# Four stages on one core: another order of GpSimd's and VectorE's steps, the last samples' work as an order written out by hand, and the filter's spectrum in five steps

## The chip, the cores and the metric

The kernel runs on one core of a Trainium2 chip. Time is device microseconds of one execution, start to end; the number compared is the median of the runs.

## What is computed

Eight samples of 512 tokens by 128 channels pass through four stages, and each stage adds the layer norm of its result to its input:

```python
x = x + _layernorm(_L0_attn_ref(_layernorm(x), ...))   # six layers
x = x + _layernorm(_L0_ffn_ref(_layernorm(x), ...))    # spiking
x = x + _layernorm(_L1_attn_ref(_layernorm(x), ...))   # state space
x = x + _layernorm(_L1_ffn_ref(_layernorm(x), ...))    # gated
```

- Stage 1: six layers of linear attention with eight heads (softmax of the queries over a head's 16 channels, of the keys over the tokens) and a leaky-ReLU feed-forward of width 512.
- Stage 2: `h = relu(x Wfc)^2`, `y = h Wproj`, then the number of spikes of a leaky integrator in five steps, which is a count of how many of five levels `y` exceeds.
- Stage 3: `u = x Win + b`, a causal convolution of each channel with a kernel built from 64 states, done through a spectrum (transform, product, inverse), and `y Wout + b`.
- Stage 4: with the token before, `xk = mu_k x + (1 - mu_k) x_prev` and `xr` likewise; `out = sigmoid(xr Wr) * (relu(xk Wk)^2 Wv)`.

## The kernel before

Everything is in fp32 and stays in on-chip memory between load and store. `X` holds the eight samples and `XI` the running input of stage 1. Each of the five engines has its own program, written in order; semaphores join them. PSUM has eight banks, each with a fixed role: `pXT`, `pQ`, `pK`, `pX2`, `pH` (two), `pY`, `pW`.

Stage 1 is a pipeline over 48 items (six layers by eight samples). In step `n`, item `n` does its keys and queries, item `n-1` its attention, item `n-2` its second norm, item `n-3` its feed-forward. Product after product is placed on TensorE so that something else runs while a result goes over ScalarE or VectorE. In a step, GpSimd does: the join of the statistics (`join`), the power that gives the second norm's scale (`RSTD`, L790), the subtraction of the queries' maximum (`QB`, L877), the power for the first norm of the next item (`RSTD`, L797), and the queries' division (`QB`, L886). VectorE begins a step with the second scaling (`XR2`, L1315), then the scaled merge (`MM`, L1477), then the transpose of the queries' blocks (`QS`, L1481), then `XTL` (L1484). ScalarE scales the next item's input (`XR`, L956) once L797 has run, and TensorE transposes that at the start of the next step.

From step 44 on, the later stages of the samples come in. Sample `v` is at stage `k` of ten in step `44 + v + k`: `at(n, k, operation)` calls it. So one sample enters with each step and all five engines' orders repeat, up to step 60. The waits that guard the reuse of a bank come from `freed(name, count)` with a formula over the step.

Beside this, the convolution's kernel is built during stage 1: GpSimd and ScalarE make 16 chunks of powers, TensorE multiplies two slices of them in each of 32 steps (`kernel_slice`) into `pW`, ScalarE copies them out in steps 41 and 42, `CENTRE` is step 43, and VectorE combines them (`butterfly`) up to step 46. The filter's spectrum, 18 products of 128x128, is made in steps 48 and 49 into `pK` and `pQ`.

In stage 4, the previous token's part is folded into the weights: `WK1 = mu_k Wk`, `WK2 = (1 - mu_k) Wk`, and TensorE multiplies both with the sample `SH`, the second shifted by a token:

```python
mm(pY[:, :], WK1[:, :], SH[:, 1:1 + SEQ], True, False)
mm(pY[:, :], WK2[:, :], SH[:, 0:SEQ], False, True)
```

## Time and profile before

| | |
|---|---|
| time, three runs | 846.48, 844.92, 845.98 us; median 845.98 |
| profiled execution | 846.16 us, of which 844.3 from the first to the last instruction |
| mean granted TensorE clock | 0.981 |
| busy | TensorE 791.0 us (94%), VectorE 662.4 (78%), ScalarE 584.7 (69%), GpSimd 462.1 (55%) |

A matmul of fp32 is two rows in the profile (`x` counts them), so the 32 rows of `SH,WK` are 16 products. An `Lnnn` is a line of the kernel; helpers (`mm` is L317, `transposes` L327, `stats` L1194 and L1197, ScalarE's `copy` L908 and `normalise` L913) have one line for many uses, and the tile names tell them apart. Names lose their numbers: `XR2` reads `XR`, `WK1` reads `WK`; tiles that share the large buffer read `BIG`. Step 44 begins at 552.5 us, where GpSimd divides item 43's queries; step 48 begins at 626 us.

### The profile page before, as it was taken

How to read it: one execution, taken by the hardware profiler on the slowest of the kernel's cores; microseconds unless marked ns; L12 is line 12 of the kernel's file. 1: busy time of each engine (PE TensorE's matmuls, PEld its weight loads, DVE VectorE, ACT ScalarE, POOL GpSimd, SP SyncE). 2: the span in 40 equal slices, each digit the busy share in tenths (PEclk: the TensorE clock that was granted, in tenths of full speed). 3: DMA queues.
4: the chain of work that ended last, by engine and by line, in shares of the span. 5: the costliest groups of instructions: out<-in, count | busy, mean ns of one | idle time of the engine just before them, and what ended most of it. 6: DMA issues, size and time to landing. Idle time of an engine off the chain costs nothing.

```text
span 844.3 us, 16194 instructions
## 1 busy us (share of the span) xinstructions
PE 791.0 (94%) x5354; PEld 687.8 (81%) x5354; DVE 662.4 (78%) x1937; ACT 584.7 (69%) x1244; POOL 462.1 (55%) x740
## 2 busy tenths in 40 slices
PE   7689999999999999999999999989999999998864
PEld 3468888999899989999899998878888887877752
DVE  4668788888788788788878787897875799999951
ACT  3466777787787777777777777778777657756353
POOL 6888556565576536544554445543454355566543
PEclk9799999999999999999999999999999999999996
DMA  9200000100000000100001000000000000000001
GB/s 258 94 0 2 1 1 1 39 1 2 1 26 14 2 2 1 38 2 1 1 2 39 1 1 1 1 1 3 1 1 1 2 1 2 2 14 26 14 14 38
DMA packets 19729, 13.70 MB, mean 16 GB/s; under 512 B 2488, under 2 KB 18495, under 8 KB 19647
## 3 DMA queue, kind: packets, MB, share of 16 engines
q1 hardware_dynamic: 19646, 12.67, 5.2%
q8 instruction: 44, 0.72, 0.4%
q14 instruction: 39, 0.31, 0.1%
HBM read 10.57 MB, written 2.10 MB: 15 GB/s over the span
## 4 chain that ended last, share of the span: by engine, by line
PE 76%; POOL 9%; DVE 7%; issue 4%; ACT 3%; DMA 0%; POOLq 0%; ACTq 0%; DVEq 0%
PE PS L317 68%; PE PS L327 8%; POOL XI L767 2%; ACT BIG L913 1%; POOL QB L877 1%; POOL RSTD L790 1%; POOL RSTD L797 1%; POOL RX L758 1%; ACT XR L956 1%; DVE QSM L1537 1%; DVE STATS L1273 1%; DVE STX L1258 1%; POOL R L725 1%; DVE ST L1194 0%; DVE XR L1315 0%
## 5 line engine op out<-in xcount | busy, mean ns | idle before, releaser
L317 PEld LDWEIGHTS PS<-W,HL 128*128 128x128 f32 x1536 | 194.1, 191 | 13.3 <-issue 5.3
L317 PE MATMUL PS<-W,HL 128*128 128x128 f32 x1536 | 202.0, 275 | 0.0
L969 ACT ACTIVATE HL<-PS 128x512 f32<-128x512 f32 x192 | 109.3, 593 | 14.5 <-PE PS L317 10.6
L779 POOL TENSOR_TENSOR JOIN<-STATS 128x8 f32<-128x8 f32 (+1 forms) x48 | 12.2, 254 | 159.0 <-DVE STATS L1273 159.0
L317 PE MATMUL PS<-X2H,W1L 128*128 128x512 f32 x192 | 91.6, 477 | 2.6 <-issue 2.2
L1138 ACT ACTIVATE EK<-PS,NKM 128x512 f32<-128x512 f32 x48 | 33.0, 688 | 76.7 <-DVE NKM L1498 76.7
L886 POOL TENSOR_TENSOR QB<-QB,QRC 128x512 f32<-128x512 f32 x48 | 50.9, 1061 | 56.5 <-DVE QRC L1540 56.5
L956 ACT ACTIVATE XR<-XI,RSTD 128x128 f32<-128x128 f32 x192 | 61.5, 393 | 25.4 <-POOL RSTD L797 25.3
L317 PE MATMUL PS<-X2H,W1H 128*128 128x512 f32 x192 | 76.2, 397 | 0.0
L317 PE MATMUL PS<-X2L,W1H 128*128 128x512 f32 x192 | 76.0, 396 | 0.0
L1273 DVE BATCH_NORM_STATS2 STATS<-XI 128x6 f32<-128x128 f32 x352 | 75.5, 277 | 0.1
L327 PE MATMUL PS<-ID,XR 128*128 128x128 f32 x384 | 61.2, 283 | 9.4 <-ACT XR L956 9.4
L724 POOL TENSOR_SCALAR VE<-MV 128x4 f32<-128x4 f32 x56 | 13.5, 241 | 102.8 <-DVE MV L1197 101.4
L725 POOL TENSOR_TENSOR R<-VE,MHALF 128x4 f32<-128x4 f32 x56 | 59.8, 1069 | 4.7
L1509 DVE STREAM_TRANSPOSE QB<-QF 128x512 f32<-128x512 f32 x48 | 34.2, 712 | 34.5 <-ACT QF L908 34.5
L317 PE MATMUL PS<-MM,QS 128*128 128x128 f32 x384 | 54.7, 286 | 4.3 <-DVE MM L1477 2.8
L327 PEld LDWEIGHTS PS<-ID,XR 128*128 128x128 f32 x384 | 44.4, 144 | 15.1 <-ACT XR L956 12.4
L797 POOL TENSOR_TENSOR RSTD<-JOIN,MHALF 128x4 f32<-128x4 f32 x40 | 55.2, 1381 | 0.0
L1495 DVE TENSOR_TENSOR XI<-PS,XI 128x512 f32<-128x512 f32 x48 | 33.1, 690 | 27.6 <-PE PS L317 27.6
L317 PEld LDWEIGHTS PS<-MM,QS 128*128 128x128 f32 x384 | 47.6, 194 | 8.2 <-DVE MM L1477 4.5
L877 POOL TENSOR_TENSOR QB<-QB,QMX 128x512 f32<-128x512 f32 x48 | 51.7, 1078 | 4.5 <-DVE QMX L1513 4.5
L1320 DVE TENSOR_TENSOR X2L<-X2F,X2H 128x512 fp32r<-128x512 f32 x48 | 36.0, 749 | 23.2 <-ACT X2F L961 23.1
(215 smaller groups left out, 2167.2 us busy)
## 6 DMA issues: line engine op xcount, KB each, us to landing
W<-in_w SPq DMA_DIRECT2D x12, 256.0 KB
X<-in_x SPq DMA_DIRECT2D x8, 256.0 KB, 4.6
out<-X SPq DMA_DIRECT2D x8, 256.0 KB, 2.3
QKV<-in_qkv SPq DMA_DIRECT2D x6, 192.0 KB, 2.8
FWD<-in_fwd SPq DMA_DIRECT2D x1, 1024.0 KB, 5.5
INV<-in_inv SPq DMA_DIRECT2D x1, 1024.0 KB, 8.1
WO<-in_wo SPq DMA_DIRECT2D x6, 64.0 KB
FWDX<-in_fwdx SPq DMA_DIRECT2D x1, 256.0 KB, 6.5
```

Source lines behind the costliest of these rows:

```text
L317: return nc.tensor.matmul(o, l, r, start=start, stop=stop, skip_group_check=True)
L327: last = nc.tensor.transpose(o[:, j * P:(j + 1) * P], i[:, j * P:(j + 1) * P], ID[:, :])
L725: return pool.tensor_tensor(RS[k][:, :], VES[k][:, :], MHALF[:, 0:TILES], ALU.pow)
L797: power = pool.tensor_tensor(RSTD[:, 0:TILES], variance, MHALF[:, 0:TILES], ALU.pow)
L877: pool.tensor_tensor(heads(QB[:, :]), heads(QB[:, :]), QMX[:, :].unsqueeze(2).broadcast_to([P, 32, DH]), ALU.subtract).then_inc(s["q_sub"], 1)
L886: pool.tensor_tensor(heads(QB[:, :]), heads(QB[:, :]), QRC[:, :].unsqueeze(2).broadcast_to([P, 32, DH]), ALU.mult).then_inc(s["q_nrm"], 1)
L956: last = nc.scalar.activation(o[:, j * P:(j + 1) * P], tile(src, b, j), ACT.Copy, scale=r[:, first + j:first + j + 1])
L969: nc.scalar.activation(HL[f][:, :], pH[f % 2][:, :], ACT.Prelu, alpha=LEAK).then_inc(s["hl"], 1)
L1273: last = nc.vector.bn_stats(STATS[:, first + j, :], tile(src, b, j))
L1320: tt(X2L[:, :], X2F[:, :], X2H[:, :].bitcast(FP32), ALU.subtract).then_inc(s["x2l"], 1)
L1495: tt(xo, pQ[:, :], xo, ALU.add).then_inc(s["resid1"], 1)
L1509: nc.vector.transpose(QB[:, :], QF[:, :]).then_inc(s["q_blk"], 1)
```

## The change

- GpSimd, each step of stage 1: the first norm's power comes right behind the join, and the second norm's power behind the queries' subtraction.
- VectorE, each step: merge and `QS` come ahead of the second scaling.
- Three kernel slices a step instead of two, so the kernel is complete in step 30; `CENTRE` is step 33, and the spectrum is made in steps 37 to 41, two units a step, all into `pW`.
- From step 44 on, the loop over steps ends. Each engine has a written-out list of calls for what is left, with the counts that guard a bank beside the call. A sample no longer enters with each step: samples 1 and 2 come close together, as do 4 and 5, and the last items' feed-forwards are taken as fast as they come.
- Stage 4: the mixture with the previous token is made on the activations. ScalarE copies the transposed sample twice, scaled by `1 - mu` (`SHK`, `SHR`), and VectorE adds `mu x` from PSUM in two instructions (`blend`). TensorE then multiplies once, not twice: one product fewer of 512 columns and four fewer of 128 for each sample.
- The normed results go into `XI` in place of five separate tiles, so some waits on their reuse go. The output's weight and bias of stage 3 have their mean taken out once, so its norm only scales.

The core of the difference, with the lists cut to TensorE's last lines:

```diff
-SLICES = {DECAY + 3 + i: 2 * i for i in range(PAIRS // 2)}
-KERNEL_OUT = DECAY + 3 + PAIRS // 2
+SLICES = {DECAY + 3 + i: 3 * i for i in range(1 + PAIRS // 3)}
+KERNEL_OUT = DECAY + 4 + PAIRS // 3
 CENTRE, CENTRE_IN = KERNEL_OUT + 2, KERNEL_OUT + 3
-SPECTRUM = {ITEMS: (0, 1, 2, 3), ITEMS + 1: (4, 5, 6, 7, 8)}
+SPECTRUM = {CENTRE + 4 + i: (2 * i, 2 * i + 1)[:1 if i == TILES else 2] for i in range(TILES + 1)}
...
-                mm(pY[:, :], WK1[:, :], SH[:, 1:1 + SEQ], True, False)
-                mm(pY[:, :], WK2[:, :], SH[:, 0:SEQ], False, True).then_inc(s["k2_ps"], 1)
+                mm(pY[:, :], WKT[:, :], XK[:, :]).then_inc(s["k2_ps"], 1)
...
-                    mm(pXT[:, j * P:(j + 1) * P], SH[:, 1 + j * P:1 + (j + 1) * P], WR1[:, :], True, False)
-                    last = mm(pXT[:, j * P:(j + 1) * P], SH[:, j * P:(j + 1) * P], WR2[:, :], False, True)
+                    last = mm(pXT[:, j * P:(j + 1) * P], XM[:, j * P:(j + 1) * P], WRT[:, :])
...
+            def step(n, b, layer):
+                join(n)
+                run(first_root, n + 1)
+                run(queries_shift, n)
+                run(second_root, n - 1)
+                run(queries_scale, n)
...
-                copy(SH[:, 1:1 + SEQ], pX2[:, :]).then_inc(s["sh_T"], 1)
+                nc.scalar.activation(SHK[:, 1:1 + SEQ], pX2[:, :], ACT.Copy, scale=NMU[:, 1:2])
+                nc.scalar.activation(SHR[:, 1:1 + SEQ], pX2[:, :], ACT.Copy, scale=NMU[:, 0:1]).then_inc(s["sh_T"], 1)
...
+            def blend(v):
+
+                dve.wait_ge(s["sh_T"], v + 1)
+                if some(v):
+                    dve.wait_ge(s["k2_ps"], v)
+                    dve.wait_ge(s["r_ps"], v)
+                stt(out=XK[:, :], in0=pX2[:, :], scalar=MU[:, 1:2], in1=SHK[:, 0:SEQ], op0=ALU.mult, op1=ALU.add)
+                stt(out=XM[:, :], in0=pX2[:, :], scalar=MU[:, 0:1], in1=SHR[:, 0:SEQ], op0=ALU.mult,
+                    op1=ALU.add).then_inc(s["blend"], 1)
...
+            def step(n, b, layer):
+                run(scaled_merge, n - 1)
+                run(queries_out, n - 1)
+                run(second_scale, n - 2)
+                run(stream_low, n)
...
+            gate(3, u_sum=8); shift_turn(4, blend=4); key(3, rv=3); project_out(6, r_relu=4)
+            transform(7, 0, back=7); transform(7, 1, back=7); value(3, o_sum=7); inverse(7); gate(4, r_sig=4)
+            key(4, rv=4); shift_turn(5, blend=5); project_out(7, r_relu=5); value(4, o_sum=8); key(5, rv=5)
+            shift_turn(6, blend=6); gate(5, r_sig=5); value(5, r_relu=6); gate(6, r_sig=6); key(6, rv=6)
+            shift_turn(7, blend=7); value(6, r_relu=7); gate(7, r_sig=7); key(7, rv=7); value(7, r_relu=8)
```

GpSimd in a step of stage 1, before: the two `RSTD` rows are the powers of the second norm and then of the first, the two `QB` rows the queries' subtraction and division.

```order
L785 TENSOR_TENSOR JOIN<-JOIN 128x8
L790 TENSOR_TENSOR RSTD<-JOIN,MHALF 128x4
L877 TENSOR_TENSOR QB<-QB,QMX 128x512
L797 TENSOR_TENSOR RSTD<-JOIN,MHALF 128x4
L886 TENSOR_TENSOR QB<-QB,QRC 128x512
```

The same place of the changed kernel, where L767 is the first norm's power and L760 the second's:

```order
L749 TENSOR_TENSOR JOIN<-JOIN 128x8
L767 TENSOR_TENSOR RSTD<-JOIN,MHALF 128x4
L772 TENSOR_TENSOR QB<-QB,QMX 128x512
L760 TENSOR_TENSOR RSTD<-JOIN,MHALF 128x4
L777 TENSOR_TENSOR QB<-QB,QRC 128x512
```

The two powers have changed places around the subtraction; nothing was added.

VectorE at the start of a step of stage 1, before (`XR` is the second scaling, `QS` the queries' blocks):

```order
L1315 TENSOR_TENSOR XR<-XI,RSTD 128x512
L1477 SCALAR_TENSOR_TENSOR MM<-PS,KRC,BM 128x128
L1481 STREAM_TRANSPOSE QS<-QB 128x512
L1484 TENSOR_TENSOR XTL<-XTF,XTH 128x512
L1495 TENSOR_TENSOR XI<-PS,XI 128x512
```

And in the changed kernel:

```order
L1345 SCALAR_TENSOR_TENSOR MM<-PS,KRC,BM 128x128
L1352 STREAM_TRANSPOSE QS<-QB 128x512
L1318 TENSOR_TENSOR XR<-XI,RSTD 128x512
L1359 TENSOR_TENSOR XTL<-XTF,XTH 128x512
L1364 TENSOR_TENSOR XI<-PS,XI 128x512
```

The second scaling went two places back; `XTL` still follows both.

TensorE at the very end, before: from sample 6's value on, the turn of sample 7 (`ID,BIG`), its key (`SH,WK`), its gate (`WR,SH`) and its value (`WVT,BIG`).

```order
L317 MATMUL PS<-WVT,BIG 128x128 x3
L327 MATMUL PS<-ID,BIG 128x128
L327 MATMUL PS<-ID,BIG 128x128 x3
L317 MATMUL PS<-SH,WK 128x512
L317 MATMUL PS<-SH,WK 128x512
L317 MATMUL PS<-WR,SH 128x128
L317 MATMUL PS<-WR,SH 128x128 x7
L317 MATMUL PS<-WVT,BIG 128x128
L317 MATMUL PS<-WVT,BIG 128x128 x3
```

In the changed kernel, from sample 6's gate on (`WRT,BIG` is a gate, `BIG,WKT` a key, `ID,XI` a turn):

```order
L307 MATMUL PS<-WRT,BIG 128x128
L307 MATMUL PS<-WRT,BIG 128x128 x3
L307 MATMUL PS<-BIG,WKT 128x512
L317 MATMUL PS<-ID,XI 128x128
L317 MATMUL PS<-ID,XI 128x128 x3
L307 MATMUL PS<-WVT,BIG 128x128
L307 MATMUL PS<-WVT,BIG 128x128 x3
L307 MATMUL PS<-WRT,BIG 128x128
L307 MATMUL PS<-WRT,BIG 128x128 x3
L307 MATMUL PS<-BIG,WKT 128x512
L307 MATMUL PS<-WVT,BIG 128x128
L307 MATMUL PS<-WVT,BIG 128x128 x3
```

The second product of a key and four of the eight of a gate are gone, and sample 7's turn goes ahead of sample 6's value.

## Rows read from the trace of the kernel before

**Rows 1.** The page's chain that ended last, share of the span by engine

```profile
PE 76%; POOL 9%; DVE 7%; issue 4%; ACT 3%; DMA 0%; POOLq 0%; ACTq 0%; DVEq 0%
```

**Rows 2.** Windows: busy time of each engine in steady state and three stretches of the end

```profile
240.00:480.00 240.00, 239.37 (x1726) 218.61 (x1725) 194.37 (x461) 180.05 (x372) 123.93 (x192) 1.00 0.04 11
552.50:626.00 73.50, 71.30 (x467) 60.52 (x466) 59.46 (x194) 54.78 (x115) 32.53 (x55) 0.98 0.01 1
626.00:813.80 187.80, 176.71 (x1177) 148.57 (x1175) 160.87 (x633) 118.91 (x275) 98.26 (x165) 0.99 0.03 8
813.80:844.30 30.50, 13.69 (x60) 9.71 (x60) 7.08 (x35) 12.14 (x27) 13.01 (x24) 0.74 0.09 27
```

**Rows 3.** Windows inside 626 to 800 us

```profile
626.00:680.00 54.00, 53.75 (x365) 45.69 (x364) 38.27 (x156) 36.04 (x78) 21.30 (x35) 1.00 0.01 1
680.00:740.00 60.00, 59.90 (x402) 50.19 (x402) 56.53 (x226) 42.19 (x98) 35.82 (x59) 1.00 0.01 1
740.00:800.00 60.00, 51.85 (x346) 43.54 (x346) 56.33 (x221) 33.10 (x83) 34.99 (x60) 0.97 0.06 19
```

**Rows 4.** Groups of TensorE by form: busy us, mean ns, idle before

```profile
L317 PE MATMUL PS<-SH,WK 128*128 128x512 f32 x32 | 18.7, 714 | 1.6 <-DVE BIG L1442 0.8 <-ACT SH L908 0.8
...
L317 PE MATMUL PS<-WR,SH 128*128 128x128 f32 x128 | 16.0, 279 | 0.0
...
L317 PE MATMUL PS<-KV,FWD 128*128 128x128 f32 x28 | 3.4, 275 | 0.0
```

**Rows 5.** Groups of VectorE by form, the same columns

```profile
L1315 DVE TENSOR_TENSOR XR<-XI,RSTD 128x512 f32<-128x512 f32 x48 | 50.4, 1050 | 0.0
...
L1477 DVE SCALAR_TENSOR_TENSOR MM<-PS,KRC,BM 128x128 f32<-128x128 f32 x48 | 16.3, 339 | 0.0
...
L1442 DVE TENSOR_TENSOR BIG<-PS,BOUT 128x512 f32<-128x512 f32 x8 | 5.5, 682 | 0.3
```

**Rows 6.** Timeline of GpSimd and ScalarE, a steady step at 304 us

```profile
304.56 1.01 POOL L790 TENSOR_TENSOR RSTD<-JOIN,MHALF 128x4 f32<-128x4 f32 x1
...
306.55 1.46 POOL L797 TENSOR_TENSOR RSTD<-JOIN,MHALF 128x4 f32<-128x4 f32 x1
...
308.04 1.28 ACT L956 ACTIVATE XR<-XI,RSTD 128x128 f32<-128x128 f32 x4 [0.78 <-POOL RSTD L797]
```

**Rows 7.** Timeline of all engines, 552 to 556 us

```profile
552.42 1.06 POOL L886 TENSOR_TENSOR QB<-QB,QRC 128x512 f32<-128x512 f32 x1 [2.38 <-DVE QRC L1540]
...
552.80 1.23 DVE L1315 TENSOR_TENSOR XR<-XI,RSTD 128x512 f32<-128x512 f32 x1
...
553.96 0.34 DVE L1477 SCALAR_TENSOR_TENSOR MM<-PS,KRC,BM 128x128 f32<-128x128 f32 x1
...
554.22 0.69 DVE L1481 STREAM_TRANSPOSE QS<-QB 128x512 f32<-128x512 f32 x1
```

**Rows 8.** Waits between 20 and 130 us: total, times, longest

```profile
PE PS L327 <- ACT XR L956: 7.9, 7, 2.3
...
ACT XR L956 <- POOL RSTD L797: 3.3, 7, 0.8
```

**Rows 9.** Timeline of the last 43 us, all engines

```profile
801.43 1.88 PE L317 MATMUL PS<-SH,WK 128*128 128x512 f32 x4
...
813.81 0.69 DVE L1442 TENSOR_TENSOR BIG<-PS,BOUT 128x512 f32<-128x512 f32 x1
...
826.99 0.60 ACT L908 ACTIVATE SH<-PS 128x512 f32<-128x512 f32 x1 [1.27 <-PE PS L327]
...
827.73 3.75 PE L317 MATMUL PS<-SH,WK 128*128 128x512 f32 x4 [0.78 <-ACT SH L908]
...
833.48 1.06 PE L317 MATMUL PS<-WVT,BIG 128*128 128x128 f32 x8
```

**Rows 10.** Windows around 750 us; the third number from the end is PEclk

```profile
740.00:750.00 10.00, 7.89 (x63) 6.76 (x63) 9.79 (x41) 5.46 (x15) 5.22 (x13) 1.00 0.10 28
750.00:760.00 10.00, 10.00 (x49) 7.40 (x49) 9.49 (x36) 5.85 (x15) 7.40 (x9) 0.83 0.00 1
```

More of the change, by code:

```diff
@@ new lines, in context, with values @@
+            def context(i, **readers):
+                held(readers)
+                if late(i):
+                    freed("ek", i + 1, readers)
+                pe.wait_ge(s["ek_tm"], i + 1)
+                for j in range(TILES):
+                    last = mm(pK[:, 0:P], XR[:, j * P:(j + 1) * P], EKT[:, j * P:(j + 1) * P], j == 0, j == TILES - 1)
+                last.then_inc(s["g_ps"], 1)
+            def values(i):
+                pe.wait_ge(s["wv"], i // BATCH + 1)
+                pe.wait_ge(s["gt"], i + 1)
+                mm(pK[:, P:2 * P], WV[slot(i)][:, :], GT[:, :]).then_inc(s["c_ps"], 1)
@@ L602, in step @@
-                if b == 0 and has_n:
-                    value_bias(layer)
-                if sample(n, 1) is not None:
-                    freed("ym", passed(n - 1, 1))
-                    spiking_second(sample(n, 1), 0)
-                if has_m:
-                    freed("relu", FB * passed(n, 1) - 2)
-                    freed("relu", FB * passed(n - 1, 1))
-                    h(m, 3)
+                run(attend, n - 1)
+                run(keys, n)
+                run(second, n - 3, 1)
@@ L641, in step @@
+                run(second_turn, n - 2)
+                run(second, n - 3, 2)
+                run(context, n)
                 if n == 0:
                     keep_busy(2)
[L643 to L650 removed]
@@ new lines, in _ @@
+            spiking_first(0, 0, hl=175); second_turn(44, in_T=1); second(43, 2); spiking_first(0, 1, hl=176)
+            context(46, ek=47); second(43, 3); values(46); spiking_first(0, 2, relu=1); spiking_first(0, 3, relu=2)
+            hidden(44, 0, relu=3); spiking_second(0, 0); spiking_second(0, 1); spiking_second(0, 2)
+            spiking_second(0, 3); merge(46); hidden(44, 1, relu=4); turn(47, ek_tm=47); spiking_turn(1, x2h=45)
+            hidden(44, 2, hl=177); second(44, 0, resid2=44); attend(46, q_fm=47); keys(47, m_ready=47)
@@ new lines, in _ @@
+            project_in(3, cnt_z=5); shift_turn(0, in_T=7); spiking_second(5, 2); spiking_second(5, 3); inverse(2)
+            spiking_first(6, 0, relu=23); spiking_first(6, 1, relu=24); gate(0, u_sum=4); key(0, o_sum=2)
+            count(5, r_sig=1); spiking_first(6, 2, relu=25); state_turn(4, blend=1); project_out(2, r_relu=1)
+            transform(3, 0, back=3); spiking_turn(7, st_T=5); spiking_first(6, 3, relu=26); value(0, o_sum=3)
+            transform(3, 1, back=3); project_in(4, cnt_z=6); spiking_second(6, 0, ym=6); spiking_second(6, 1)
@@ new lines, in _ @@
+            spiking_first(7, 0, relu=27); spiking_second(6, 2); spiking_second(6, 3); shift_turn(1, in_T=8)
+            inverse(3); key(1, rv=1); gate(1, u_sum=5); state_turn(5, blend=2); spiking_first(7, 1, relu=28)
+            count(6, r_sig=2); spiking_first(7, 2, relu=29); transform(4, 0, back=4); project_out(3, r_relu=2)
+            transform(4, 1, back=4); spiking_first(7, 3, relu=30); spiking_second(7, 0, ym=7); spiking_second(7, 1)
+            project_in(5, cnt_z=7); spiking_second(7, 2); spiking_second(7, 3); inverse(4); count(7, u_sum=6)
@@ L769, in input_norm, with join_parts @@
                 last.then_inc(s["xi_init"], 1)
-            def join(first, end, turn):
+            def join_parts(first, end, turn):
                 def part(i):
```

979 lines of the change are left out of this document (484 added, 495 removed).

## The prediction, on record before the changed kernel was timed

> **What bounds the kernel now.** I read the chain that ended last first: TensorE holds 76% of it, with GpSimd, VectorE and ScalarE sharing most of the rest [rows 1]. That says who bounds on average, not where. The windows say where [rows 2]. In 240 us of stage 1, TensorE is busy for 239.4 and VectorE for 194.4: nothing that another engine does earlier can shorten that stretch. From 552.5 us on, where the later stages come in, there are three pieces. Steps 44 to 47 (73.5 us) still belong to TensorE with 71.3 busy. The middle, 187.8 us up to the last sample's output sum, has TensorE at 176.7 and VectorE at 160.9, that is 94% and 86%. The last 30.5 us is one sample's chain, with TensorE at 13.7 and VectorE at 7.1. Cutting the middle finer [rows 3], VectorE has slack up to 680 us (38.3 of 54), then runs at 94% of 120 us (56.5 and 56.3 of 60 each), while TensorE falls from 59.9 to 51.9 of 60. So the middle changes its bound at about 740 us: first TensorE, while VectorE idles for want of samples; then VectorE, while TensorE idles.
>
> **The change, part by part.** The sum is made against the profiled execution, 846.16 us, of which 1.9 lie outside the span of 844.3. The median of the runs is 0.2 lower, so the two can be read as one.
>
> *Orders in stage 1.* The first norm's power no longer waits behind the second's and the subtraction. In the steady step shown, `XR` stood for 0.78 us for that power, which itself took 1.46 [rows 6]. The steady stretch has 0.6 us of TensorE idle in 240, so the gain there is nothing, covered by TensorE. In the first 130 us TensorE does wait: 7.9 us for `XR` in seven waits, while `XR` in turn waited 3.3 us for the power [rows 8]. Only the 3.3 can go: between 0 and 3.3, and I take 3.3, since `QS` comes earlier too and the 7.9 leaves room. The power of the second norm is now late by one subtraction, but its reader runs in the next step. On VectorE, `MM` and `QS` come ahead of the second scaling. `XTL` still has both in front of it, so only `QS` gains, about 0.7 us a step, and TensorE hides that in the steady part. What queues behind `QS` if the division is late is `XR2`, and its turn on TensorE is half a step away.
>
> The trace shows one thing more here. The second scaling took 1.23 us where it ran beside GpSimd's division [rows 7], and 1.05 in the mean of 48, against 0.68 for an addition of the same size with one operand in PSUM [rows 5]. The Trainium skill (GPSIMD Engine Reference, Specifications) says that GpSimd shares its SBUF interface with VectorE and contends with instructions that have two SBUF inputs, and the trace agrees. By that rule the scaling, now behind `QS`, runs after the division and costs about 0.68, which takes 0.37 from each step of VectorE; by the rows nothing of it reaches the time while TensorE is full, so the sum is the same by both.
>
> *The spectrum.* 14 of its 18 products are 3.4 us in the groups [rows 4], so 18 are 4.4 us. They leave steps 48 and 49 and enter steps 37 to 41, which TensorE fills: plus 4.4 before step 44, minus 4.4 behind it. The kernel slices stay the same in number.
>
> *Stage 4's products.* 16 key products of 512 columns take 18.7 us and 64 gate products 16.0 [rows 4], so a sample's loses one key product (1.17) and four of 0.25. The key figure holds slow-clock time: at full clock two took 1.88 [rows 9], so between 0.94 and 1.17. I take 1.0 and 1.0, 16 us in all. In return VectorE gets two instructions a sample. None of before mixes a PSUM and an SBUF tensor with a scalar at 512 columns. Bounds: 0.34, the same operation at 128 columns, and 1.05, the slowest of 512; I take 0.68, the addition with a PSUM operand, which reads the same amount [rows 5]. That is 1.36 a sample and 10.9 in all (5.4 to 16.8). ScalarE gets one more copy of 0.6 a sample; it is at 119 of 188 in the middle and hides it.
>
> *The written-out end.* TensorE from 552.5 on was 71.3 + 176.7 + 13.7 = 261.7 [rows 2]; less 16 and 4.4 that is 241.3. VectorE was 59.5 + 160.9 + 7.1 = 227.4; with the blend 238.3. I split both over the same three pieces.
> - Steps 44 to 47. The list gives TensorE the same four items and three first halves of the spiking stage; three second products of 1.0 go and one count comes. About 69.5 busy. TensorE-bound, 71 us where 73.5 were; of the 2.2 us idle before I leave 1.5. VectorE about 60.
> - The end, from sample 7's output sum. TensorE: four values, three gates, three keys of 1.0 and two turns of about 0.65, 11.3. VectorE: in 30.5 us before, three sums or products and four statistics made 7.1, so a statistic is 1.26; now five, six, and six blends of 0.68, 15.0. The chain: two blends and one copy more, 1.36 + 0.6. From the first key product to the value were 5.75 us at the slow clock [rows 9]; with half the products (and relu, square and sigmoid between) I estimate 4.2. That is 0.4 more, and 0.6 for three samples in flight where there were two: 31.5.
> - The middle. What is left: TensorE 241.3 - 69.5 - 11.3 = 160.5, VectorE 238.3 - 60 - 15.0 = 163.3. The two are even, so the length is the work over how full the fuller is kept. VectorE kept 94% between 680 and 800, and 71% before, where samples came one a step. The lists bring samples 1 and 2 in together and 4 to 6 early, which removes the lack. At 94%: 174 us, where 187.8 were.
>
> Sum: 552.5 + 4.4 - 3.3 + 71 + 174 + 31.5 = 830.1, and with 1.9 outside the span 832.0.
>
> **The rivals.** A median of three moves by about 0.2% here, 1.7 us, so that is what I call no change.
> - *Forecast* (0.55): VectorE 92 to 96% full in the middle, 170 to 177.5 us, with a microsecond or two on either side elsewhere: 826 to 838.
> - *Both engines fit together* (0.13): the middle comes to TensorE's own bound, 160.5 over the 99.8% that it had from 680 to 740, or 163.3 over 97%: 161 to 168 us, 819 to 826. For it: VectorE's order in the middle has many independent pieces. Against: to fill both, neither may wait for the other.
> - *The list packs no better* (0.20): VectorE stays at the 86% of the whole middle before: 163.3/0.857 = 190.5, and time 848.6; at 89% it is 183.5 and 841.5. Work taken from TensorE would then only make it wait more, since the stage behind the items belongs to VectorE. For it: the blend goes onto the engine that is full from 680 on. Against: the 86% came from 54 us without samples. I give 0.13 to 838 to 844.3 and 0.07 to no change.
> - *Slower: the transposes' bank* (0.09). All turns write `pX2`. Before, it came free after one copy, 0.6; now after two copies and two blends, 0.6 + 0.6 + 1.36 = 2.56 and whatever is queued on VectorE ahead of the blend. The next turn and the gate stand on TensorE for it, and everything behind them stands too. From 832 it takes more than 1.95 us at each of eight samples to reach 847.7, and at 3 us each the time is 856. Against: in the list, most blends have an inverse or several first products between them and the next user of the bank; only samples 5 to 7 have two short products there.
> - *The clock* (0.03). TensorE idled for 2.1 of 10 us, and in the next 10 us the granted clock was 0.83 [rows 10]; in the last piece it was 0.74, and two keys took 3.75 us instead of 1.88 [rows 9]. Each such spell costs some 1.7 us. With TensorE at 160.5 of 174, or 92%, two or three more could come: 3 to 5 us, time 835 to 837. The Trainium skill (TensorE: Matmul & The Clock Gate, What's actually happening) has the array at 1.2 GHz after idling and 2.4 GHz when busy; by that rule a middle with short waits alone would stay at full clock, and the time would stay at 832.
>
> **How the numbers follow.** Likeliest 832. Faster: 0.55 + 0.13 + 0.13, and the 0.03 of the clock's own case, 0.84. Same 0.07, slower 0.09. The range leaves out 0.04 below and 0.16 above: the unknown price of the blend alone (5.4 to 16.8) moves the sum by -6 to +6, the head by 3.3. That gives 821 to 844. The likeliest case's own range is 826 to 838.
>
> **What the profile after would show.** Step 44 starts at about 553.6 (up 4.4, down 3.3). Step 48 some 71 us later. TensorE's busy sum falls by some 16 us, to 775, with 16 rows each of the key and 64 of the gate. VectorE's rises by 11 less what the second scaling loses, and its windows behind step 48 read 94%. The two blend instructions take 0.68 each. The forecast is wrong if VectorE's windows there stay below 90%, if turns or gates on TensorE wait for the blend by over a microsecond each, or if steps of stage 1 are longer than before because the second norm's power is late.

## The result and the profile after

The changed kernel takes 843.18 us in the median of 20 runs (842.1 to 846.45), the kernel before 846.15 on the same chip (20 runs, 844.57 to 850.1). The ratio is 0.9965, with a 95% interval of 0.9954 to 0.9975: faster, beyond the 1.7 us that the prediction calls no change, but by 3 us where 14 were forecast. 832 was predicted; 843.2 lies inside the range of 821 to 844 and far outside the likeliest case's own.

The windows of the profiled execution (span 841.6), for the same four pieces as in [rows 2]; after the busy times stand PEclk, the DMA share and GB/s:

```profile
240.00:480.00 240.00, 236.48 (x1706) 216.43 (x1704) 192.27 (x476) 176.81 (x369) 117.53 (x192) 1.00 0.04 11
559.70:629.20 69.50, 68.66 (x452) 56.92 (x451) 55.78 (x195) 55.07 (x118) 36.22 (x59) 1.00 0.01 1
629.20:809.80 180.60, 163.69 (x1062) 137.07 (x1060) 165.59 (x611) 108.68 (x259) 83.83 (x136) 0.97 0.02 6
809.80:841.60 31.80, 13.18 (x70) 9.58 (x70) 14.98 (x59) 19.45 (x45) 18.38 (x32) 0.78 0.15 42
```

Set beside the forecast, piece by piece. The borders are `MM` of items 43 and 47 and the last output sum:

| piece | before | forecast | after |
|---|---|---|---|
| `MM` of item 43 starts | 554.0 | 555.1 | 559.7 |
| four items, to `MM` of item 47 | 72.1 | 69.6 | 69.5 |
| the middle | 187.7 | 174 | 180.6 |
| the end | 30.5 | 31.5 | 31.8 |

So two terms hold, and two miss: the head by 4.6 us, the middle by 6.6. The middle cut finer, as in [rows 3]:

```profile
629.20:680.00 50.80, 50.80 (x355) 43.29 (x354) 45.24 (x167) 29.04 (x67) 21.86 (x37) 1.00 0.01 1
680.00:740.00 60.00, 57.71 (x374) 46.91 (x373) 57.21 (x223) 45.55 (x109) 28.46 (x46) 1.00 0.01 1
740.00:800.00 60.00, 46.77 (x301) 40.56 (x300) 55.53 (x188) 29.23 (x74) 30.28 (x45) 0.94 0.05 13
```

VectorE is 95% full from 680 to 740 us, as forecast, and 93% afterwards, while TensorE, with less to do, stands more than before. The waits of TensorE in the middle, in total, times, longest:

```profile
PE PS L307 <- DVE BIG L1515: 7.9, 5, 2.9
PE PS L307 <- DVE BIG L1499: 5.7, 3, 2.8
...
PE PS L307 <- DVE BIG L1540: 0.3, 1, 0.3
```

L1515 is the last instruction of `back_bands`, L1499 the last sum of `spectra`, L1540 the blend. The waits are for the work on samples, hardly for the blend: the rival of the turned bank is false. The groups of VectorE and TensorE that answer to [rows 4, 5] (busy us, mean ns, idle before):

```profile
L1318 DVE TENSOR_TENSOR XR<-XI,RSTD 128x512 f32<-128x512 f32 x48 | 36.8, 766 | 0.0
L1498 DVE TENSOR_TENSOR BIG<-BIG 128x512 f32<-128x512 f32 x8 | 8.8, 1098 | 0.5
L1499 DVE TENSOR_TENSOR BIG<-BIG 128x512 f32<-128x512 f32 x8 | 7.6, 953 | 0.0
L1540 DVE SCALAR_TENSOR_TENSOR BIG<-PS,MU,SHR 128x512 f32<-128x512 f32 x8 | 5.9, 741 | 0.0
```
```profile
L307 PE MATMUL PS<-BIG,WKT 128*128 128x512 f32 x16 | 9.4, 673 | 2.8 <-DVE BIG L1548 2.4 <-DVE BIG L1540 0.3
L307 PE MATMUL PS<-WRT,BIG 128*128 128x128 f32 x64 | 9.1, 287 | 2.1 <-DVE BIG L1471 1.1 <-DVE BIG L1540 1.0
```

The products' price was right: 18.5 us where 34.7 were, 16.2 less. The blend takes 0.73 and 0.74 an instruction, 11.7 in all (0.68 and 10.9 forecast). The second scaling fell from 1.05 to 0.77, most of the way to the 0.68 forecast.

### The profile page after: what moved, and what is told of

The parts are those of the page before. It is cut to its first block, busy times and chain, and to the rows that moved or that the text cites. A ratio compares the mean times of both kernels' runs of the same rounds, so it can differ in the third digit from the quotient of the medians.

```text
span 841.6 us, 16091 instructions
## 1 busy us (share of the span) xinstructions
PE 777.2 (92%) x5274; PEld 677.6 (81%) x5274; DVE 666.8 (79%) x1957; ACT 579.2 (69%) x1252; POOL 446.5 (53%) x724
## 4 chain that ended last, share of the span: by engine, by line
PE 67%; DVE 17%; POOL 8%; issue 5%; ACT 2%; DMA 0%; POOLq 0%; DVEq 0%; ACTq 0%
PE PS L307 61%; PE PS L317 7%; POOL XI L731 3%; DVE ST L1196 2%; DVE QSM L1395 1%; POOL RX L722 1%; POOL QB L772 1%; DVE BIG L1499 1%; DVE MV L1199 1%; POOL RSTD L767 1%; DVE XR L1318 1%; ACT XI L886 1%; DVE XTL L1359 1%; DVE STX L1260 1%; DVE XI L1369 1%
## 5 line engine op out<-in xcount | busy, mean ns | idle before, releaser
L743 POOL TENSOR_TENSOR JOIN<-STATS 128x8 f32<-128x8 f32 (+1 forms) x48 | 12.0, 250 | 176.3 <-DVE STATS L1275 176.3
L307 PE MATMUL PS<-X2H,W1L 128*128 128x512 f32 x192 | 88.7, 462 | 3.1 <-issue 2.8
L317 PE MATMUL PS<-ID,XR 128*128 128x128 f32 x384 | 58.5, 275 | 9.6 <-ACT XR L929 9.6
L934 ACT ACTIVATE XTH<-PS,LNC,SC 128x512 fp32r<-128x512 f32 x48 | 37.4, 778 | 41.1 <-PE PS L317 41.1
L760 POOL TENSOR_TENSOR RSTD<-JOIN,MHALF 128x4 f32<-128x4 f32 x48 | 60.9, 1268 | 0.2
L1385 DVE STREAM_TRANSPOSE QB<-QF 128x512 f32<-128x512 f32 x48 | 34.1, 711 | 31.1 <-ACT QF L881 31.1
L307 PE MATMUL PS<-EKT,XR 128*128 128x128 f32 x384 | 51.0, 276 | 1.6 <-ACT EKT L881 1.6
```

The lines of the kernel that those rows point to most:

```text
L307: return nc.tensor.matmul(o, l, r, start=start, stop=stop, skip_group_check=True)
L317: last = nc.tensor.transpose(o[:, j * P:(j + 1) * P], i[:, j * P:(j + 1) * P], ID[:, :])
L760: pool.tensor_tensor(RSTD[:, TILES:2 * TILES], JOIN[:, 4, TILES:2 * TILES], MHALF[:, TILES:2 * TILES], ALU.pow).then_inc(s["ln2_rstd"], 1)
L934: return nc.scalar.activation(o[:, :], i[:, :], ACT.Identity, scale=SC[slot][:, which:which + 1], bias=LNC[slot][:, 2 * which + 1:2 * whic ...
L1385: nc.vector.transpose(QB[:, :], QF[:, :]).then_inc(s["q_blk"], 1)
```

## The experiments

Each was timed beside the kernel before in five rounds. The ratio is to that kernel; the changed kernel's own is 0.9965, and 0.001 is 0.85 us. The checkpoints below are from the profiled executions. Up to item 7 executions differ by up to 1.3 us (115.6 to 116.9 at `MM` of item 7), so pieces of the head are counted from item 7 on, or step by step. A layer has eight items; the long steps 15 and 16, 23 and 24, 31 and 32 are its edges. The late weights are what is tied to `CENTRE`: two products on TensorE, their copies, the `butterfly` steps, and the weights' sums and factors on VectorE.

### The clock

TensorE's rows in the changed kernel, two of the eight inverses:

```profile
745.54 3.62 PE L307 MATMUL PS<-INV,BIG 128*128 128x256 f32 x16
...
761.67 5.41 PE L307 MATMUL PS<-INV,BIG 128*128 128x256 f32 x16 [1.98 <-DVE BIG L1499]
...
799.49 5.41 PE L307 MATMUL PS<-INV,BIG 128*128 128x256 f32 x16 [2.82 <-DVE BIG L1499]
```

The same 16 instructions take 3.6 or 5.4 us, and the longer ones stand here behind waits of 2 us and more. The windows around the first of them:

```profile
750.00:760.00 10.00, 8.11 (x66) 7.37 (x65) 9.76 (x33) 5.97 (x18) 3.47 (x6) 1.00 0.01 2
760.00:770.00 10.00, 6.27 (x18) 4.48 (x18) 8.62 (x29) 3.85 (x11) 5.09 (x9) 0.83 0.00 1
```

**e1_fill_middle.** Products that nobody reads, put where TensorE would stand; nothing of the kernel's own is left out. (In the trace each is two instructions.)

```diff
+            def filler(times):
+                pe.wait_ge(s["ym"], BATCH)
+                for _ in range(times):
+                    mm(pW[:, 0:P], CE1[:, 0:P], CE1[:, 0:P])
...
-            inverse(5);
+            filler(6); inverse(5);
```

> The changed kernel with short products that nobody reads (128 columns, into a bank that is free by then) put on TensorE where it stands for VectorE late in the middle: 6 ahead of sample 5's inverse, 9 ahead of its output product, 2 and 8 for sample 6, 8 ahead of sample 7's inverse. Theory A, the clock: in the changed kernel the inverses of samples 5 and 7 took 5.4 us where the others took 3.6 to 3.7, and sample 7's forward products 5.0 where others took 3.8, all behind a wait of TensorE of 2 to 2.8 us. These excesses lie on the chain and add up to 4.8 us. With the fillers the granted clock stays at 1.00 from 750 to 805 us, the products take 3.6 and 3.8, and the time falls by 3 to 5 us against the changed kernel. Theory B, VectorE is full and takes up whatever TensorE gains: the products get shorter, the time stays within 1 us. Theory C: the fillers themselves delay the inverses: 1 to 3 us slower.

842.16 us, ratio 0.9941 (0.9921 to 0.9961), span 839.7. The middle took 178.7 us. Sample 5's inverse took 3.72 and sample 7's forward products 3.74, but sample 7's inverse again 5.41: eight fillers ended well before it. The direction of theory A, at half its size or less: 1 us by the medians, 2 us by the ratios, whose intervals overlap.

**e7_fill_all.** The same with more of them, from sample 5's inverse to the last value: 46 ahead of the last output product and 25 after it (the expectation's 62 and 29 were miscounted).

```diff
-            filler(8); inverse(7);
+            filler(14); inverse(7);
...
-            value(6, r_relu=7)
+            filler(7); value(6, r_relu=7)
```

> The changed kernel with short unread products wherever TensorE stands, from sample 5's inverse to the last value: 62 of them before the last output product, more ahead of sample 7's inverse than in the first kernel with fillers (14 for 8, where TensorE still stood for 2.1 us and then ran the inverse at half clock, 5.4 us for 3.6), and in the end piece 29. Theory A, the clock: sample 7's inverse takes 3.7, the keys and values of the end the times of full clock (0.95 us for a key), and the time is 2 to 3 us below that with the first fillers. Theory B: the end piece hangs on ScalarE's and GpSimd's norms, and only the inverse's 1.7 us comes.

840.17 us (839.82 to 840.47), ratio 0.9928 (0.9916 to 0.9940), span 837.4. The middle is 177.1, the end 31.3. Its inverse of sample 7, with 0.77 us of wait left:

```profile
797.42 3.72 PE L307 MATMUL PS<-INV,BIG 128*128 128x256 f32 x16 [0.77 <-DVE BIG L1505]
```

So work that is thrown away (11.6 us of TensorE's time in the middle) makes the kernel 3 us faster. In the profiled execution the clock costs the changed kernel 3.5 us in the middle and 0.5 in the end, which does hang on the norms, as theory B had it for that piece.

That execution lost more than most. The runs e5, e6 and e2 below edit stage 1 only and leave the middle's orders as they are; their middles took 178.6, 178.4 and 179.4 us, where the changed kernel's took 180.6 and e7's 177.1. In e5 sample 7's inverse was slow and sample 5's was not. By the medians of the times the fillers are worth 3.0 us. These traces show too that the length of a wait does not settle the clock. First e5, then e6:

```profile
761.20 3.72 PE L307 MATMUL PS<-INV,BIG 128*128 128x256 f32 x16 [1.98 <-DVE BIG L1499]
...
797.15 5.33 PE L307 MATMUL PS<-INV,BIG 128*128 128x256 f32 x16 [3.88 <-DVE BIG L1499]
```
```profile
800.82 3.72 PE L307 MATMUL PS<-INV,BIG 128*128 128x256 f32 x16 [2.42 <-DVE BIG L1499]
```

The wait of 1.98 us that was followed by 5.41 us in the changed kernel is followed by 3.72 in e5, and one of 2.42 us by 3.72 in e6.

### The head

**e4_spectrum_early.** The kernel before with the early part alone: slices, late weights and spectrum.

```diff
-SLICES = {DECAY + 3 + i: 2 * i for i in range(PAIRS // 2)}
-KERNEL_OUT = DECAY + 3 + PAIRS // 2
-SPECTRUM = {ITEMS: (0, 1, 2, 3), ITEMS + 1: (4, 5, 6, 7, 8)}
+SLICES = {DECAY + 3 + i: 3 * i for i in range(1 + PAIRS // 3)}
+KERNEL_OUT = DECAY + 4 + PAIRS // 3
+SPECTRUM = {CENTRE + 4 + i: (2 * i, 2 * i + 1)[:1 if i == TILES else 2] for i in range(TILES + 1)}
```

> The kernel before with one part of the change alone: three kernel slices a step, and with that the late weights and the spectrum's products in steps 33 to 41 and in the bank of the slices, instead of steps 43 to 49. Theory A, the forecast's: step 44 starts 4.4 us later, steps 48 and 49 are 4.4 us shorter, the time is the same as before within 1 us. Theory B: in the head it costs more than the products (the late weights' work on VectorE now falls on the steps behind a layer's edge, some 1.5 us at steps 33 and 34), and behind step 48 less comes back than 4.4: 1 to 3 us slower than before.

847.68 us, ratio 1.0016 (1.0004 to 1.0028): slower than before by 1.4 us, theory B. Step 44 starts 7.3 us later than before, more than in the changed kernel. Which part the surplus comes from took two more runs.

**e13_slices_only** keeps `CENTRE` and `CENTRE_IN` at 43 and 44 and the spectrum at 48 and 49:

```diff
-CENTRE, CENTRE_IN = KERNEL_OUT + 2, KERNEL_OUT + 3
+CENTRE, CENTRE_IN = KERNEL_OUT + 12, KERNEL_OUT + 13
```

> The kernel before with three kernel slices a step (steps 9 to 30) instead of two (steps 9 to 40), the late weights and the spectrum where they were. Theory A: up to step 31 it runs 1.5 to 2 us behind the kernel before, and steps 32 to 40, now without slices, give nothing of it back, since their length is set by something else than TensorE's sum (in the kernel before, steps 41 and 42, without slices, took 11.9 and 12.1, no less than those with two): step 44 starts 1.5 to 2 us later, the time likewise. Theory B, the forecast's: their number is the same, so what the early steps pay the later ones get back: within 0.5 us at step 44.

847.74 us, ratio 1.0022 (1.0009 to 1.0035).

**e14_slices_centre** has the late weights early too:

```diff
-CENTRE, CENTRE_IN = KERNEL_OUT + 12, KERNEL_OUT + 13
+CENTRE, CENTRE_IN = KERNEL_OUT + 2, KERNEL_OUT + 3
```

> As the run before, with the late weights too in steps 33 to 36 (where they were: steps 43 to 46), the spectrum's products still in steps 48 and 49. Theory A: steps 33 and 34, behind a layer's edge, become 2.1 us longer together, and step 43 gets 0.9 back; step 44 starts another 1 us later than with the slices alone, and steps 44 to 46 take 2 us less. Against the kernel with the spectrum early too (step 44 at 561.2) the spectrum's own price in the head is then 4.2 to 4.4 us. Theory B: the late weights are free early (other engines have room there), and the spectrum alone costs 5 us or more, more than its products.

847.50 us, ratio 1.0016 (1.0002 to 1.0029). The ladder by the start of `MM`, in us behind the kernel before:

| `MM` of item | slices only | and late weights | and spectrum | changed kernel |
|---|---|---|---|---|
| 7 | 0.8 | 0.1 | 0.0 | 0.5 |
| 8 | 0.8 | 0.1 | 0.0 | -0.7 |
| 31 | 2.7 | 2.0 | 1.9 | 1.2 |
| 36 | 2.7 | 4.1 | 4.0 | 3.5 |
| 43 | 2.5 | 3.1 | 7.3 | 5.8 |
| 47 | 2.6 | 0.2 | 4.3 | 3.2 |

Slices: the steady step goes from 11.87 to 11.93 us, step 17 from 11.92 to 12.86, and steps 32 to 40, freed of slices, stay as they were (11.86 to 12.93) within 0.01. Step 25, which stands to the next edge as 17 does to its own, only goes from 11.91 to 11.98 with the same slice more; what makes step 17 dear is open. A slice more costs, a slice less gives nothing back: 1.9 us lost up to item 31, of which 0.2 comes back in step 42 (ScalarE's copies of the kernel moved too, from steps 41 and 42 to 31 and 32) and 1.7 is lost for good. The late weights: 0.85 and 0.97 us more in steps 33 and 34; then 0.85, 1.66 and 1.28 less in steps 43 to 45. Counted from item 7, they lose 1.3 up to item 43 and are 1.7 ahead at item 47; the table's 0.6 and 2.4 hold 0.7 of scatter in the first steps. The spectrum: 4.2 us in steps 37 to 41, and 3.9 back in the middle, 188.1 to 184.2. That term held.

**e2_scaling_first.** The changed kernel with the second scaling ahead again on VectorE.

```diff
-                run(scaled_merge, n - 1)
-                run(queries_out, n - 1)
                 run(second_scale, n - 2)
+                run(scaled_merge, n - 1)
+                run(queries_out, n - 1)
```

> The changed kernel with one edit undone: on VectorE, in every step of stage 1, the second norm's scaling stands again ahead of the scaled merge and the queries' transpose. Theory A: before, the scaling filled the time in which VectorE had to wait for GpSimd's division anyway; now VectorE stands for the division (10.9 us over 48 items) and the scaling comes on top, ahead of the low part of the turned stream for which TensorE waits at the layers' edges. Undone, the start of step 44 comes 2 to 3 us earlier, and the scaling's mean goes from 0.77 us back to about 1.05. Theory B: TensorE is full in stage 1 and hides either order: within 0.5 us. Theory C, the change's reason: the queries' transpose is what the next product waits for, and undone the kernel is 1 us or more slower.

844.93 us, ratio 0.9989 (0.9976 to 1.0002): 2 us slower than the changed kernel, `MM` of item 43 at 561.5 instead of 559.7. Theory A, mine, is false: the wait that the change put in front of `QS` costs less than the scaling there. The scaling's group in this run, and VectorE's waits in the changed kernel and in this run:

```profile
L1318 DVE TENSOR_TENSOR XR<-XI,RSTD 128x512 f32<-128x512 f32 x48 | 48.0, 1000 | 0.0
```
```profile
DVE QS L1352 <- POOL QB L777: 10.9, 29, 0.4
```
```profile
DVE QS L1352 <- POOL QB L777: 0.7, 2, 0.4
```

10 us of waiting went, 11.2 us of scaling beside GpSimd's division came, and each `QS` starts a scaling later. The scaling does cover the wait, and it is still the worse order.

**e6_power_back.** The changed kernel with GpSimd's old order:

```diff
-                run(first_root, n + 1)
-                run(queries_shift, n)
                 run(second_root, n - 1)
+                run(queries_shift, n)
+                run(first_root, n + 1)
                 run(queries_scale, n)
```

> The changed kernel with one edit undone: on GpSimd, in every step of stage 1, the second norm's power stands again ahead of the queries' subtraction, and the first norm's power behind it. Theory A, from the head's numbers (the first 116 us are as long in both kernels): this order is worth nothing, within 0.5 us, though ScalarE's waits for the power come back (25 us in all). Theory B, the forecast's: 3.3 us slower, in the first 130 us. Theory C: the second norm's power came too late in the changed kernel, since VectorE now scales in the same step: undone, it is 1 us or more faster.

843.93 us, ratio 0.9975 (0.9965 to 0.9986): 0.8 us slower. `MM` of item 7 comes at 116.9 instead of 116.0, and of item 31 at 410.3 instead of 408.9. Counted from item 7 on, item 43 comes 0.95 later. The order is worth about 1 us, between theories A and B, and theory C is false; the times alone, with overlapping intervals, would not show it.

**e5_centring_later.** The seven small instructions of the mix factors and the centring move to step 42.

```diff
-                if n == CENTRE_IN:
+                if n == ITEMS - 6:
                     dve.wait_ge(s["late_in"], LATE_LOADS)
                     ts(NMU[:, :], MU[:, :], -1.0, 1.0, ALU.mult, ALU.add)
```

> The changed kernel with one edit: VectorE's seven small instructions that turn the mix factors round and centre the output weights and bias (1.6 us) run in step 42 instead of step 34. Theory A: in step 34, right behind a layer's edge, they stand between the second norm's copy and its low part, TensorE stood for 1.6 us there and the step took 13.2 us where steps without such work take 11.9; moved to step 42, which TensorE fills, step 34 loses 1 to 1.6 us, step 42 stays at 11.5, and the time falls by 1 to 1.6 us against the changed kernel. Theory B: another thing of the step (the kernel's first butterflies, 1.1 us on the same engine) is the cause: within 0.3 us at step 34.

842.60 us, ratio 0.9967 (0.9953 to 0.9982): no change in the time. In the trace step 34 fell from 13.18 to 11.78 us, as theory A had it, and steps 42 and 43 rose by 0.81 and 0.36: TensorE did not hide them there. First the changed kernel, then this one:

```profile
442.27 0.78 ACT L934 ACTIVATE X2F<-PS,LNC,SC 128x512 f32<-128x512 f32 x1
...
443.70 0.17 DVE L1421 TENSOR_SCALAR NMU<-MU 128x2 f32<-128x2 f32 x1
...
445.26 0.68 DVE L1325 TENSOR_TENSOR X2L<-X2F,X2H 128x512 fp32r<-128x512 f32 x1
...
446.04 0.48 PE L307 MATMUL PS<-X2H,W1L 128*128 128x512 f32 x1 [1.62 <-issue]
```
```profile
443.77 0.69 DVE L1325 TENSOR_TENSOR X2L<-X2F,X2H 128x512 fp32r<-128x512 f32 x1
...
444.56 0.47 PE L307 MATMUL PS<-X2H,W1L 128*128 128x512 f32 x1
```

**e9_fill_centring** puts e5 and e7 together; it is the base of the rest.

> The changed kernel with both earlier edits: the unread products wherever TensorE stands late, and the centring in step 42. It is the base of the next three. Theory: the clock stays up, so the runs lie within 1 us of each other, as they did with the fillers alone (839.8 to 840.5); the middle takes 177 us, and the head's edit gives 0.3 to 1 us more: 839.3 to 840.

839.21 us, ratio 0.9918 (0.9903 to 0.9932), span 837.2; the middle 177.1, the end 31.4. As expected.

### The blend

**e3_no_blend.** The changed kernel with two weight matrices for key and for gate, and one plain copy of the turned sample.

```diff
-                mm(pY[:, :], WKT[:, :], XK[:, :]).then_inc(s["k2_ps"], 1)
+                mm(pY[:, :], SHR[:, 0:P], SHK[:, 1:1 + SEQ], True, False)
+                mm(pY[:, :], SHR[:, P:2 * P], SHK[:, 0:SEQ], False, True).then_inc(s["k2_ps"], 1)
```

> The changed kernel without the blend: two weight matrices each for key and gate as before the change, one plain copy of the turned sample on ScalarE, and on VectorE no blend. The lists are otherwise the same. TensorE gets 16 to 19 us more, VectorE 11.8 us less. Theory A, VectorE was the bound of the middle and the blend moved work onto it: what TensorE gained it could not use; the middle comes to 173.8 us of TensorE at 97 to 98%, some 178 to 180 us where the changed kernel has 180.6, and the time is within 2 us of the changed kernel's. Theory B, the forecast's: the blend bought the middle more than it cost; without it 6 us or more slower than the changed kernel.

846.57 us, ratio 0.9997 (0.9984 to 1.0010), 2.7 us slower than the changed kernel. It was no clean price: the weights' own sums, now at step 34, made the head 2.3 us longer, and the middle (180.9) had its own spells of the slow clock. What is left for the rest of the kernel is 0.5 us by the ratios, 1 by the medians.

**e10_fill_no_blend.** The same on the base, weight sums in step 42.

> The base without the blend: key and gate with two weight matrices each again, the four weight sums in step 42. It prices the blend with the clock and the head held still. Theory A: in the middle the blend is worth nothing, since VectorE was the bound there (the middle within 1 us of the base's 177), and in the end piece, where both keys, all gates and no full engine are on the chain, 1.8 us: 1.5 to 2.5 us slower than the base. Theory B, the forecast's: TensorE's 16 us count, 5 us or more slower.

844.69 us, ratio 0.9979 (0.9968 to 0.9990), 5.5 us slower than the base (5.6 in the spans): 1.2 in the head (0.4 of it before item 7, the rest the weights' sums in step 42), 3.4 in the middle, 1.0 in the end. By the number theory B. The middle of the base and of this one:

```profile
628.70:805.80 177.10, 168.95 (x1156) 144.05 (x1155) 166.59 (x611) 108.68 (x259) 84.41 (x136) 1.00 0.02 6
```
```profile
629.90:810.40 180.50, 176.30 (x1206) 150.50 (x1205) 162.74 (x602) 105.60 (x253) 84.48 (x137) 1.00 0.02 6
```

Without the blend the engines are busy at 98% and 90%; with it VectorE has 94%. But 11.6 of TensorE's 176.3 us are the fillers, placed for the gaps of the base. Where this run has no such gap they stand in front of the kernel's own products (the output product behind the fillers at 789.72 us starts without a wait, where the base's waits 0.66), so 5.5 us is an upper figure for the blend. e3 points the same way: four of its twelve runs, at the highest granted clock of the twelve (0.987 to 0.989), took 844.4 to 844.8 us, about as long as this run, without a filler and with item 47 of its trace 1.4 us later. Behind item 47 the blend is worth 0.5 to 1 us as the kernels stand and 4.4 with the fillers in both; that TensorE bounds the middle when it has the old products is not shown.

### The contention and the end

**e8_small_adds.** GpSimd's sums of the residual stream over 128 columns instead of 512; the rest of each sum is left out.

```diff
-                pool.tensor_tensor(seq(X, v), seq(X, v), seq(XI, v), ALU.add).then_inc(s["cnt_x"], 1)
+                pool.tensor_tensor(tile(X, v, 0), tile(X, v, 0), tile(XI, v, 0), ALU.add).then_inc(s["cnt_x"], 1)
```

> The changed kernel with GpSimd's 24 sums of the residual stream cut to a quarter, 128 columns of 512; three quarters of each sum are left out, so this prices them only. Theory A, contention: VectorE's sums of the spectra (1.10 and 0.95 us in the mean, up to 1.75 beside a sum on GpSimd) fall to 0.68 each, which takes 5.5 us off VectorE in the middle, and with the sums' own length off the chains (0.9 each) the middle falls from 180.6 to about 174 us, the forecast's figure. Theory B: VectorE's extra time is not on the chain: the durations fall, the time by under 2 us.

837.01 us, ratio 0.9889 (0.9873 to 0.9905); the middle 174.9, the end 31.1. The sums of the spectra:

```profile
L1499 DVE TENSOR_TENSOR BIG<-BIG 128x512 f32<-128x512 f32 x8 | 6.0, 752 | 0.0
...
L1498 DVE TENSOR_TENSOR BIG<-BIG 128x512 f32<-128x512 f32 x8 | 5.8, 727 | 0.5
```

Theory A, but the shorter sums also shorten the chains, so it does not price contention alone.

**e11_psum_spectra.** The base with the imaginary products of samples 5 to 7 in PSUM.

```diff
-                tt(PI[:, :], pQ[:, :], KIM[:, :], ALU.mult)
-                tt(PR[:, :], pQ[:, :], KRB[:, :], ALU.mult).then_inc(s["pr_im"], 1)
+                pi, pr = (pH[0], pH[1]) if v >= 5 else (PI, PR)
+                tt(pi[:, :], pQ[:, :], KIM[:, :], ALU.mult)
+                tt(pr[:, :], pQ[:, :], KRB[:, :], ALU.mult).then_inc(s["pr_im"], 1)
```

> The base with the imaginary products of samples 5 to 7 in two PSUM banks that the spiking stage has left, instead of in SBUF, so that the sums of the spectra have one operand each in PSUM. Same instructions, same sizes. Theory A, contention with GpSimd over SBUF: a sum with one operand in PSUM is not slowed by GpSimd's sum beside it (products and sums with a PSUM operand took 0.67 to 0.68 us throughout); the six sums fall to 0.68 each, some 2.5 to 3 us off VectorE, and the time falls by 2 us. Theory B: writing the products into PSUM costs what the reading saves, or the chain goes by another way: within 0.5 us.

837.32 us, ratio 0.9895 (0.9879 to 0.9912), 2 us below the base, all in the middle (175.1). Theory A: same instructions, same sizes, and none of the six sums is slowed. Of samples 0 to 4, whose operands both stay in SBUF, two sums still take 1.7 to 1.8 us.

```profile
L1509 DVE TENSOR_TENSOR BIG<-BIG,PS 128x512 f32<-128x512 f32 x3 | 2.0, 680 | 0.0
L1508 DVE TENSOR_TENSOR BIG<-BIG,PS 128x512 f32<-128x512 f32 x3 | 2.0, 677 | 0.2
```

Sample 5's sums beside GpSimd's, in the changed kernel and in this one: GpSimd's sums run at the same place in both.

```profile
758.13 1.27 POOL L800 TENSOR_TENSOR X<-X,XI 128x512 f32<-128x512 f32 x1 [1.62 <-ACT XI L886]
758.22 1.73 DVE L1498 TENSOR_TENSOR BIG<-BIG 128x512 f32<-128x512 f32 x1
...
759.36 1.71 POOL L816 TENSOR_TENSOR X<-X,XI 128x512 f32<-128x512 f32 x1
...
759.87 1.75 DVE L1499 TENSOR_TENSOR BIG<-BIG 128x512 f32<-128x512 f32 x1
```
```profile
757.60 1.28 POOL L806 TENSOR_TENSOR X<-X,XI 128x512 f32<-128x512 f32 x1 [1.62 <-ACT XI L892]
757.70 0.69 DVE L1508 TENSOR_TENSOR BIG<-BIG,PS 128x512 f32<-128x512 f32 x1
758.30 0.68 DVE L1509 TENSOR_TENSOR BIG<-BIG,PS 128x512 f32<-128x512 f32 x1
...
758.83 1.27 POOL L822 TENSOR_TENSOR X<-X,XI 128x512 f32<-128x512 f32 x1
```

**e12_own_tiles.** The base with own tiles and banks for the last two samples.

```diff
-                tt(ACC[:, :], pY[:, :], SIG[:, :], ALU.mult).then_inc(s["rv"], 1)
+                acc = {6: PI, 7: PR}.get(v, ACC)
+                tt(acc[:, :], pY[:, :], SIG[:, :], ALU.mult).then_inc(s["rv"], 1)
...
-                mm(pY[:, :], WKT[:, :], XK[:, :]).then_inc(s["k2_ps"], 1)
+                bank = pY if v < 6 else pH[v % 2]
+                mm(bank[:, :], WKT[:, :], XK[:, :]).then_inc(s["k2_ps"], 1)
```

> The base with tiles of their own for the last two samples: the key's product in banks of the spiking stage instead of the value's bank, and the gated product in two tiles of the spectra instead of the one shared. Theory A, the end is a loop over samples: in the changed kernel each of the last three gated products waits for the norm of the one before (5.8 us a sample, of which the last stood 2.9 us after its value was there); with own tiles the end piece falls by 2 to 3 us. Theory B: ScalarE's order holds it to the old pace: under 1 us.

837.84 us, ratio 0.9902 (0.9886 to 0.9918); the end 30.2 instead of 31.4. The loop was real, but only 1.2 us deep. VectorE's waits for ScalarE's norm (L886 and L893) in the end, of the changed kernel and of this one:

```profile
DVE BIG L1548 <- ACT XI L886: 5.2, 3, 3.8
```
```profile
DVE BIG L1557 <- PE PS L307: 3.1, 2, 2.7
...
DVE BIG L1557 <- ACT XI L893: 0.8, 1, 0.8
```

**e15_all_edits** joins the base with both; no further edit.

> The base (unread products where TensorE stands late, centring in step 42) with both the imaginary products in PSUM and the last two samples' own tiles. Theory A, the causes are independent: -2.0 in the middle and -1.2 in the end, 835.9 us. Theory B: one hides the other: 837 or more.

836.08 us, ratio 0.9884 (0.9868 to 0.9901); the middle 175.1, the end 30.2. They add up.

**e16_weights_off_edge** shifts the late weights and the spectrum two steps:

```diff
-CENTRE, CENTRE_IN = KERNEL_OUT + 2, KERNEL_OUT + 3
+CENTRE, CENTRE_IN = KERNEL_OUT + 4, KERNEL_OUT + 5
```

> The run before with the late weights two steps later, 35 to 38, and the spectrum in steps 39 to 43. Theory A, the layer's edge makes them dear: steps 33 and 34 fall from 13.4 and 11.8 to about 12.9 and 11.6, steps 35 and 36 rise by less; step 44 starts 0.5 to 1 us earlier. Theory B: it is TensorE's two products (1.0 and 0.4 us) and costs the same wherever it stands: within 0.3 us.

834.87 us (834.72 to 835.20), ratio 0.9868 (0.9852 to 0.9884). Steps 33 and 34 fell from 13.43 and 11.77 to 12.56 and 11.56, step 35 rose by 0.46, and `MM` of item 43 comes 0.9 us earlier (1.2 counted from item 7): theory A. It is the fastest version: 1.3% below the kernel before, 1.0% below the changed one.

## Why the prediction was wrong, step by step

**The head** (4.4 - 3.3 = 1.1 forecast, 5.8 measured). The spectrum's 4.4 was right: 4.2. Three steps failed.
- "The kernel slices stay the same in number": as a sum of work it was right, as time it was not. Three a step cost 1.9 us, and the steps that they left gave nothing back; 1.7 are left at item 43.
- The late weights had no term at all. They move with `CENTRE`, ahead of my checkpoint: 1.3 up to item 43. The surplus behind a layer's edge is the same mistake as with the slices, work on a step that has no room.
- The orders were to give 3.3 in the first 130 us. From item 7 on, the head of the changed kernel is 1.9 us shorter than that of the kernel before with the early part alone: 1.1 in step 8, 0.8 after step 31. By single edits, counted the same way, the scaling's order is worth 2.1 and the power's 0.95, by the times 2.0 and 0.8; the new weights' centring takes 1.4 back at step 34. I had looked for the gain in the power, and taken VectorE's order to be hidden by TensorE, the scaling's shorter time with it.

1.7 + 1.3 + 4.2 - 1.9 = 5.3 from item 7 on, and 0.5 before it, which is within the scatter of the first steps.

**Steps 44 to 47** (2.5 less forecast, 2.6 measured). The number held by luck, the reason did not. I gave it to the lists; the kernel before with only the late weights moved away already gains 2.9 here (72.1 to 69.2).

**The middle** (174 forecast, 180.6 measured). Two things failed.
- The clock: I called it a rival with 0.03, at 3 to 5 us. It was the case: 3.5 us of 6.6 in the profiled execution, shown by e7 against the changed kernel; 1.3 to 2.3 in the traces of e5, e6 and e2, and 3.0 in the median of the times with the end's part. TensorE with 16 us less to do and VectorE as bound stands 2 to 3 us at a time, and behind three of the four longest waits of the middle (1.98, 2.44 and 2.82 us) products ran in part at the lower clock; behind that of 2.89 they did not. The Trainium skill (TensorE: Matmul & The Clock Gate, What's actually happening) has the array slow after idling; the trace agrees in that the slow products stand behind waits. My reading of it, that short waits leave the clock up, failed: waits of 1.98 and 2.82 us were followed by inverses of 5.41 us instead of 3.62, and in e5 the same wait of 1.98 by one of 3.72.
- VectorE's work in it: 163.3 forecast, 166.6 in the base. With the clock held up the fill was the one forecast: 166.6 of 177.1 is 94%; in the changed kernel it was 165.6 of 180.6, 92%. The whole of VectorE's work from step 44 on was even below the forecast, 236.4 of 238.3 (55.8 + 165.6 + 15.0); I had put 60 of it in steps 44 to 47, where 55.8 came. The 3.3 us too much in the middle over 94% are 3.5 us of its length.

3.5 + 3.5 is 7.0, for the 6.6 missing; 163.3 over 94% is 173.7, which the forecast rounded up. The time of 843.2 lies where the prediction put *the list packs no better* (838 to 844.3), but that rival's VectorE, 86 to 89% full, is not what the trace has.

**What held.** TensorE's saving (16.2 of 16), the blend's price (0.74 for 0.68), the end (31.8 of 31.5), the bank's rival false (0.3 us of waits for the blend in the middle), the second scaling rid of GpSimd's division (1.05 to 0.77), and the blend as a gain, of which 5.5 us is the upper figure. I had used the contention only for the scaling, and put its worth at nothing; e2 shows 2 us for the whole order, and what part of them is the contention was not tried apart. The same contention sits in the sums of the spectra on the chain, 2 us for three samples. The Trainium skill (GPSIMD Engine Reference, Specifications) names instructions with two SBUF inputs; e11 agrees: with one input in PSUM a sum takes 0.68 us throughout.

How much of the 3 us the lists alone brought was not tried apart: from the kernel with the early part (184.2 in the middle) to the changed kernel without the blend (e3, 180.9) are 3.3 us, in which the slow clock of both and the new tiles are too.

## What to carry to other kernels

Where a change takes work from TensorE and leaves another engine as the bound, look up how long TensorE will stand at a time, and give the lower clock behind the long waits a term of its own (here up to 1.8 us behind each); unread products in the gaps were worth as much here as the whole change. Steps of a pipeline are not interchangeable: one more slice cost a steady step 0.06 us, one of two like steps behind a layer's edge 0.94 and the other 0.07, and a step that loses one may not get shorter; so a part that is moved is priced at both places, and everything that moves with its constant counts. Where a sum with both inputs in SBUF runs beside another engine's and takes 1.75 us for 0.68, as here, put one operand of it into PSUM.
